# Values of two head pairs from each loaded block of tokens, in one attention stage of a fused block

## The reference, cut to what matters

```python
qkv = x @ w_qkv.T
q, k, v = np.split(qkv, 3, axis=-1)           # 16 heads of 64; q scaled by 64 ** -0.5
# five coarser levels: q and k averaged over pairs of tokens, v summed over pairs
for lvl, (ql, kl, vl) in enumerate(levels):
    # level 0: causal scores inside blocks of 16 tokens
    # level > 0: the odd block of each pair attends to the even block before it
    A = exp(S - S.max(-1))
    Ysum += repeat(A @ v, 2 ** lvl)            # only from the last token of each group on
    Asum += repeat(A.sum(-1), 2 ** lvl)
out = (Ysum / (Asum + 1e-8)) @ w_out.T + b_out
x = x + out
```

## Time and profile before

| what | us |
|---|---|
| runs, median (lowest to highest of 3) | 561.32 (560.02 to 562.15) |
| the profiled execution | 560.87 |
| its span, first to last instruction | 559.1 |
| TensorE busy, 6408 matmul records | 506.0 (91%) |
| TensorE weight loads, beside it | 307.2 (55%) |
| VectorE busy | 425.8 (76%) |
| ScalarE busy | 291.5 (52%) |
| GpSimd busy | 250.6 (45%) |
| attention loop, iterations 0 to 14 | 226.9 to 448 |

### The profile page before, as it was taken

How to read it: one execution, slowest core, us unless ns; L and a number is a source line. 1 busy time by engine, 2 the same in 40 slices (tenths; PEclk the granted TensorE clock), 3 DMA queues, 4 the chain that set the end, 5 groups by cost and what they waited for, 6 DMA issues and landing times.

```text
span 559.1 us, 16575 instructions
## 1 busy us (share of the span) xinstructions
PE 506.0 (91%) x6408; PEld 307.2 (55%) x6408; DVE 425.8 (76%) x979; ACT 291.5 (52%) x624; POOL 250.6 (45%) x294
## 2 busy tenths in 40 slices
PE   6989888888989998999999999999999967989991
PEld 3323232356544544777767777777777755644540
DVE  3396958988747766878899888899878988847762
ACT  3644254254458864666545555546644523448870
POOL 3556677655524454252244443233333335533542
PEclk9999899998999998999999999999999987899997
DMA  6899820000269962100000000000000000169964
GB/s 182 319 426 270 94 25 0 2 0 20 66 194 277 273 211 67 31 3 21 21 21 22 22 21 22 22 21 22 22 20 9 7 2 9 40 184 277 277 215 137
DMA packets 45325, 54.09 MB, mean 97 GB/s; under 512 B 10880, under 2 KB 36416, under 8 KB 44224
## 3 DMA queue, kind: packets, MB, share of 16 engines
q1 hardware_dynamic: 42688, 47.78, 29.6%
q0 software_dynamic: 2560, 5.26, 2.7%
HBM read 43.55 MB, written 9.48 MB: 95 GB/s over the span
## 4 chain that ended last, share of the span: by engine, by line
PE 63%; DVE 22%; issue 6%; DMA 3%; ACT 3%; POOL 2%; SPq 0%; DVEq 0%; POOLq 0%; ACTq 0%
PE psum L1249 9%; PE psum L1748 7%; PE psum L1730 7%; PE psum L1821 5%; PE psum L1800 5%; PE psum L1268 4%; PE psum L1769 3%; PE psum L1256 3%; DVE arena L761 3%; POOL sorted_x L1467 2%; DVE arena L755 2%; PE psum L277 2%; PE psum L278 2%; PE psum L1007 1%; DVE arena L2030 1%
## 5 line engine op out<-in xcount | busy, mean ns | idle before, releaser
L2200 POOL TENSOR_TENSOR arena<-arena 128x512 f32<-128x512 f32 x32 | 40.9, 1302 | 110.6 <-issue 103.9
L1495 POOL DMA_INDIRECT y_tok<-arena,to x48 | 46.6, 971 | 63.3 <-ACT arena L1318 62.1
L1916 ACT ACTIVATE arena<-psum 128x512 f32<-128x512 f32 x64 | 38.1, 597 | 47.4 <-PE psum L1730 44.4
L1730 PE MATMUL psum<-arena 128*128 128x512 f32 x128 | 59.2, 605 | 0.7 <-ACT arena L1899 0.7
L1249 PE MATMUL psum<-experts,arena 128*32 x96 | 50.2, 604 | 1.1 <-ACT arena L1308 1.1
L1249 PE MATMUL psum<-arena 128*32 128x512 f32 x288 | 50.9, 605 | 0.0
L661 POOL TENSOR_TENSOR arena<-arena 128x512 f32<-128x512 f32 x32 | 37.2, 1179 | 27.9 <-DVE arena L761 17.5
L1748 PE MATMUL psum<-arena 128*128 128x128 f32 x384 | 47.5, 278 | 0.8 <-ACT arena L1921 0.8
L1748 PEld LDWEIGHTS psum<-arena 128*128 128x128 f32 x384 | 45.2, 192 | 1.8 <-ACT arena L1921 1.8
L2137 POOL TENSOR_TENSOR arena<-arena 128x256 f32<-128x256 f32 (+4 forms) x75 | 33.6, 447 | 25.9 <-ACT arena L1935 18.9
L1730 PEld LDWEIGHTS psum<-arena 128*128 128x128 f32 x128 | 22.9, 189 | 35.4 <-issue 33.8
(11 more groups left out here) (240 smaller groups left out, 1195.2 us busy)
## 6 DMA issues: line engine op xcount, KB each, us to landing
arena<-in_experts SPq DMA_DIRECT2D x48, 384.0 KB, 4.4
experts<-in_experts SPq DMA_DIRECT2D x8, 1536.0 KB, 17.3
arena<-sorted_x SPq DMA_DIRECT2D x48, 64.5 KB, 3.7
sorted_x<-zeros SPq DMA_DIRECT2D x2, 1536.0 KB, 14.3
arena<-in_w_qkv SPq DMA_DIRECT2D x16, 192.0 KB, 2.8
arena<-y_tok SPq DMA_DIRECT2D x8, 256.0 KB, 3.1
x_tok<-in_x SPq DMA_DIRECT2D x4, 256.0 KB, 4.6
arena<-in_w_out SPq DMA_DIRECT2D x16, 64.0 KB, 1.9
```

What stands on the lines that cost most here:

```text
L1495: pool.indirect_dma_start(out=y_tok, out_offset=bass.IndirectOffsetOnAxis(ap=f_to[:, s:s + 1], axis=0), in_=f_gy[(s + 4) % 8], in_offset=N ...
L1730: pe.matmul(ring("in", n, j)[:, :], b_w[n % 2][:, which * P:which * P + P], x, start=True, stop=True)\
L1916: act.activation((b_q, b_k)[which][:, part * CHUNK:part * CHUNK + CHUNK], src, ACT.Copy, scale=(D_B ** -0.5, 1.0)[which]).then_inc(h["drai ...
L2200: pool.tensor_tensor(b_yn[:, part], b_y[:, part], b_rec[:, part], ALU.mult).then_inc(h["normed"], 1)
```

## The change

TensorE multiplies each loaded block of tokens by the value weights of two neighbouring pairs at once: 12 products of 128x256 for units n and n + 1 (n even), in place of 12 of 128x128 for each unit. They stand before the loop for units 0 and 1, and in the odd iterations 1 to 13 for the next two units; the even iterations have none. An even unit is filled by 5 + 6 banks, an odd one by 5. A drain of a value bank writes two places of `b_v`. There are three places: one for even units, two in turn for odd ones.

The q and k weights of a unit come alone, the value weights of two units in a transfer of their own (`value_weights_in`). `b_yn` is gone: GpSimd multiplies y in place, in `b_y`, except for the last unit, whose y goes to `b_q` (`y_of`). `b_zt` lies in `b_s`, so `divide` now also waits for the turned fine scores. `copy_y` waits for the output products of the unit before in place of its normalisation. `b_odd` keeps only the block of levels 3 to 5 for each batch, and ScalarE's `pack` copies only these levels.

```diff
         def attention_weights_in(sp, n):
-            sp.dma_start(b_w[n % 2].rearrange("p (n c) -> p n c", c=P), w["w_qkv"][n % PAIRS]).then_inc(w_in[n % 2], 16)
+            sp.dma_start(b_w[n % 2].rearrange("p (n c) -> p n c", c=P), w["w_qkv"][n % PAIRS][:, 0:2]).then_inc(w_in[n % 2], 16)
+
+        def value_weights_in(sp, n):
+            two = w["w_qkv"][n % PAIRS:n % PAIRS + 2, :, 2:3].rearrange("u c n d -> c (n u) d")
+            sp.dma_start(b_wv.rearrange("p (u d) -> p u d", d=P), two).then_inc(wv_in, 16)
...
             if k == 0:
-                for n in range(2):
-                    attention_weights_in(sp, n)
+                attention_weights_in(sp, 0)
+                value_weights_in(sp, 0)
+                attention_weights_in(sp, 1)
...
-        b_odd, b_even = carve(TOK // 2), carve(TOK // 2)
-        B_EARLY_AT = used[0]
+        b_odd, b_even = carve(BATCH * P), carve(TOK // 2)
+        b_rec_low, b_max, b_rz = carve(CHUNK), carve(2 * TILES_B), carve(SEQ // 32)
+        B_EARLY_AT = used[0] = max(used[0], F_ROWS_AT + 2 * WROW + 4 * C)
...
-        b_w = [carve(3 * P) for _ in range(2)]
+        b_w, b_wv = [carve(2 * P) for _ in range(2)], carve(2 * P)
...
-        b_v = [carve(TILES_B * P).rearrange("p (i d) -> p i d", d=P) for _ in range(2)]
-        b_max = carve(2 * TILES_B)
-        b_zt, b_rec, b_yn = carve(SEQ), carve(SEQ), carve(SEQ)
-        b_rz = carve(SEQ // 32)
+        b_v = carve(3 * TILES_B * P).rearrange("p (u i d) -> p u i d", i=TILES_B, d=P)
+        b_zt, b_rec = b_s[:, 0:SEQ], [b_rec_low, carve(CHUNK)]
...
-        coarse_of = [[b_rec[:, 0:SEQ // 2], b_yn], [carve(SEQ // 2), carve(SEQ // 2)]]
+        coarse_of = [b_rec, [carve(SEQ // 2), carve(SEQ // 2)]]
...
+        VALUES = TILES_B // 2
+
+        def fills(n):
+            return 5 + (VALUES if n % 2 == 0 else 0)
+
+        def filled_by(n):
+            return 5 * n + VALUES * ((n + 1) // 2)
+
+        def values_of(n):
+            return b_v[:, 0 if n % 2 == 0 else 1 + n // 2 % 2]
...
+        def y_of(n):
+            return b_y if n < LAST else b_q[:, 0:SEQ]
...
             def values(n):
                 b = n // PAIRS
+                pe.wait_ge(wv_in, 16 * (n // 2) + 16)
                 for i in range(TILES_B):
-                    if i % 4 == 0:
-                        bank_free("in", n, 5 + i // 4)
+                    if i % 2 == 0:
+                        bank_free("in", n, 5 + i // 2)
                     x = b_x[:, b * SEQ + i * P:b * SEQ + i * P + P] if i < 8 else \
                         b_even[:, b * CHUNK + (i - 8) * P:b * CHUNK + (i - 8) * P + P]
-                    mm = pe.matmul(ring("in", n, 5 + i // 4)[:, i % 4 * P:i % 4 * P + P], x, b_w[n % 2][:, 2 * P:3 * P],
+                    mm = pe.matmul(ring("in", n, 5 + i // 2)[:, i % 2 * 2 * P:i % 2 * 2 * P + 2 * P], x, b_wv,
                                    start=True, stop=True)
-                    if i % 4 == 3:
+                    if i % 2 == 1:
...
-                pe.wait_ge(h["drained"], IN * n + (8 if rough else 7))
+                pe.wait_ge(h["drained"], filled_by(n // 2 * 2) + (11 if rough else 9))
...
                 if new:
                     project_last(n + 1)
-                if new:
+                if new and n % 2 == 1:
                     values(n + 1)
...
             def pack(b):
-                for level in range(1, LEVELS + 1):
+                for level in range(3, LEVELS + 1):
...
-                    after(act, h["weighed"], 2 * (n - 1) - 1 if j < 7 else 2 * (n - 1))
-                    act.activation(b_v[n % 2][:, 4 * (j - 5):4 * (j - 5) + 4, :], src.rearrange("p (i d) -> p i d", d=P),
+                    after(act, h["weighed"], 2 * (n - 1) - 1 if j < 9 else 2 * (n - 1))
+                    odd, i = 1 + n // 2 % 2, 2 * (j - 5)
+                    act.activation(b_v[:, 0:odd + 1:odd, i:i + 2, :], src.rearrange("p (i u d) -> p u i d", u=2, d=P),
                                    ACT.Copy).then_inc(h["drained"], 1)
...
 
             def copy_y(n):
                 act.wait_ge(h["weighed"], 2 * n + 2)
-                after(act, h["normed"], 2 * n)
-                act.activation(b_y, psum[:, 4 * 512:6 * 512], ACT.Copy).then_inc(h["y_out"], 1)
+                if n < LAST:
+                    after(act, h["o"], 2 * n)
...
             def divide(n):
                 dve.wait_ge(h["summed"], n + 1)
+                dve.wait_ge(h["turned"], 2 * min(n + 1, LAST) + 1)
                 dve.transpose(b_zt, psum[:, 6 * 512:8 * 512]).then_inc(h["z_out"], 1)
...
-                    after(pool, h["o"], 2 * (n - 1) + j + 1)
-                    pool.tensor_tensor(b_yn[:, part], b_y[:, part], b_rec[:, part], ALU.mult).then_inc(h["normed"], 1)
+                    pool.tensor_tensor(y_of(n)[:, part], y_of(n)[:, part], b_rec[j], ALU.mult).then_inc(h["normed"], 1)
...
-                    sp.wait_ge(h["proj"], IN * (n - 2) + IN)
+                    sp.wait_ge(h["proj"], filled_by(n - 2) + 5)
                     attention_weights_in(sp, n)
+                    if n % 2 == 0:
+                        sp.wait_ge(h["proj"], filled_by(n - 1))
+                        value_weights_in(sp, n)
```

45 lines of the change are left out of this document (24 added, 21 removed).

## The result

| what | before | changed kernel |
|---|---|---|
| runs, median (lowest to highest), 4 each | 561.63 (560.02 to 562.15) | 579.41 (578.71 to 580.20) |
| ratio, with its 95% interval | | 1.0315 (1.0281 to 1.0350) |
| the profiled execution | 560.87 | 580.01 |
| its span | 559.1 | 578.1 |
| TensorE busy | 506.0 (91%) | 509.2 (88%) |

The change costs 17.8 us by the medians. One of its six executions took 607.75 us, far above the other five (574.11 to 577.93), and is left out of the ratio. The forecast was 575.4, the range 567.5 to 580; of the first four executions one, of 580.20, lies above it.

A forecast was written before the change was run, and what follows sets the result against it. The prediction took TensorE's products to bound plain iterations, 14.20 of 14.20 us busy. Charges per pair of iterations, 3.8 + 1.3 + 1.3 + 5.6 + 2.8 - 0.4 + 0.1 = 14.5, on 560.87 gave 575.4 us, range 567.5 to 580.

The forecast's parts named there:

- TensorE pays by columns here; the weight loads are hidden.: Value products: equal columns cost equal time, 5.45 us for 12 wide ones; gain taken as 0, at best 0.9 us.
- The iteration lasts 13.3 us.: Plain short iteration, worked on iteration 8: 13.3 us instead of 14.2, saving 0.9 of the 2.8 owed.
- the own wait: In divide, VectorE's transpose of the sums waits for its own transpose of the scores: 0.12 us, bounds 0 and 0.3.
- wait (b): Before the output products of a short iteration, TensorE waits 1.0 us for GpSimd's normalised y, 0.3 more for its second half.
- (d): At the end of a short iteration, add_weights waits 0.3 us for GpSimd's merge, which starts behind the rough exponents.
- Pair 6, +1.9: Iteration 6 and its lengthened neighbour, charged together like those of iteration 8: +1.9 us.
- Iterations 4, 10 and 14 save nothing, +2.8 each: Extra VectorE statistics (10), GpSimd's bias addition (4) and routing work (14) let these short iterations save nothing: +2.8 us each.
- Edits costed at nothing: Two-place value drains, fewer packing copies, split weight transfers, normalising in place and copy_y's moved wait: 0 us.
- Short iterations that give back all: Rival: other engines run ahead in long iterations, so the waits in short ones go: 561 us, chance 6%.
- weight loads that cost time: Rival: value weight loads stand in line, so halving them saves 22.6 us: 552.8 us, chance 5%.
- Clock in all short iterations: Rival: granted clock falls to 0.83 in eight short iterations, 2.3 us each, together 18.7: 594 us, chance 4%.
- The signs: Profile if right: iterations about 17.0 and 13.3, waits before L1841, TensorE busy unchanged within 2 us, 12 value products in 5.5.

The follow-up runs named there:

- narrow_pairs: The changed kernel with each 256-column value product made as two 128-column products on the same block, so blocks are loaded twice: 576.89 us, ratio 1.0300.
- quick_norm: The changed kernel with GpSimd's normalisation of y cut to the first 64 of 512 columns of each half: 574.56 us, ratio 1.0257.
- half_turn: The changed kernel with VectorE's first transpose of divide (of the sums) cut to half its columns: ratio 1.0197.
- half_turn_before: The kernel before the change with VectorE's first transpose of divide cut to half its columns: 563.44 us beside 564.84, ratio 0.9990.
- own_sums: The changed kernel with a place of its own for the turned sums and without divide's wait for VectorE's own transpose: 575.11 us, ratio 1.0276.
- share_only: The kernel before the change with only the shared buffers and the two moved waits, value products untouched: 561.07 us beside 560.83, ratio 1.0009.
- split_values: The changed kernel with the same wide value products halved over two iterations, six blocks in the even and six in the odd one: 565.82 us, ratio 1.0107.
- the repeat: The changed kernel unaltered, measured a second time: 576.47 us beside 559.91 for the kernel before, ratio 1.0293.

## Why the prediction was right, step by step

- **"TensorE pays by columns here; the weight loads are hidden."** Right. 12 wide products took 5.45 us (224.06 to 229.51), as put; `narrow_pairs` gives 0.10 for 12 loads. I took 0 as the gain and kept 0.9 for the low end; 8 x 0.10 = 0.8 by `narrow_pairs` is nearly that end. A long iteration got 2.63 more, not 2.8 (16.84 against 14.21), and so did the stretch before the loop (2.65). Over eight of them this term was 1.4 too high.
- **"The iteration lasts 13.3 us."** 13.56, so 0.65 was saved and not 0.9. The waits in it came out as walked: 0.93 before the output products (1.0 put), their second half 0.37 longer (0.3), 0.27 before L1830 (0.3). The size of three things was off: the own wait was 0.18 and not 0.12; the rough exponents came 0.23 later and not 0.12; and the merge took 2.68 instead of 2.55.
- **What ends an iteration.** The walk was in the right order, but its reader could think that wait (b), 1.0 for GpSimd's normalisation, is the price. `quick_norm` shows that it is not. Only the last link counts, (d), and what leads to it is VectorE; `half_turn` shows that, with `half_turn_before` as its control.
- **Own wait of `divide`, 0.12 each, bounds 0 and 0.3.** `own_sums`: 0.20 to 0.23 in iterations 2, 6 and 8. Inside the bounds.
- **Iteration 0, saving 1.5.** It saved 1.74 (11.32 against 13.06); the sum with the stretch before it was +0.9 instead of +1.3.
- **Iteration 2, saving 1.5.** It saved 1.1 (13.58 against 14.67), so its pair was +1.6 instead of +1.3. The transposes of x had lengthened it by 0.46 (14.67 against 14.21) and not by the 0.62 of their row, and it now ends with the same chain as iteration 8.
- **Pair 6, +1.9.** It was +2.5. Iteration 6 lasted 14.02, 0.46 more than iteration 8, of which 0.25 is a wait at the start of iteration 7 that the prediction lacks: GpSimd packs the next batch's tokens (L2169, 333.69 to 334.92) and TensorE's projection starts at 335.02. `own_sums` and `half_turn` shorten iteration 6 as they do 8. Some 0.2 more is VectorE's later start: its fine maxima begin 0.21 us ahead of TensorE's projections here (320.76, 320.97) and 0.39 in iteration 8, while from them to TensorE's sums it is 12.92 and 12.93. Why it starts later isn't traced.
- **Iterations 4, 10 and 14 save nothing, +2.8 each (10 and 14: +2.6 with their neighbours' bank waits).** Iteration 4: +3.0. Iteration 14: +2.1. Iteration 10: +3.1 with a fall of the clock (next section), some 2.4 without it (14.98 in `narrow_pairs`, where it didn't fall there, against 15.66). Iterations 9 and 13 got 2.1 more each (16.84 against 14.71, 18.19 against 16.11), less than the 2.6 put.
- **Iteration 12, +0.1.** +0.4.
- **Edits costed at nothing.** `share_only`: 0.2 us by the medians, within its interval, though 1.0 in the loop of its one trace. The drains' double places are in `split_values` and cause no wait of note there; the transfers landed in 2.8 us as before. Those of the value weights were issued some 21 us before use and not over 25 (349.50, used at 370.42), since the load of the output weights stood ahead of them on SyncE.
- **Rivals.** Short iterations that give back all (561), and weight loads that cost time (552.8), are out. Clock in all short iterations (594): no, in one of them.
- **The signs.** Iterations of 16.84 and 13.56, the waits before L1841, the value products and the clock above 0.95 (0.99 from 230 to 440 us) came as put. TensorE's busy time rose by 3.2 us, not under 2: 1.3 of it are the output products of iteration 10 at half clock and 0.5 the router products at half clock in the last layer. The remaining 1.4 I can't place; a busy sum includes modelled ends.

The terms make 14.5 and the pairs of the table 15.5, but not because each term was right. Too low were the pairs 1 and 2 (0.3), 3 and 4 (0.2), 5 and 6 (0.6), 7 and 8 (0.1), 9 and 10 (0.5; the clock took 0.5 to 0.7 there) and 11 and 12 (0.3); too high the start (0.4) and 13 and 14 (0.5). Under them lies the same kind of offset: eight long iterations priced 1.4 too high, short ones that saved less than put. That these nearly cancel is luck; that TensorE pays in full and VectorE's chain keeps the short ones from giving it back is not. The medians say 16.6 to 17.8; what lies between these and the 15.5, 1 to 2 us, is not in the attention loop, and what of it is scatter of the other layers is left open. The first measurement, 579.4, is only 0.6 inside the range, the repeat 3.5.

## What to carry to other kernels

Moving work of a full engine between iterations at an equal sum is not free: the long iterations pay it in full, the short ones give back only down to the next chain, and the other engine's idle time of the long iteration (4.85 us here) can't be used if what it waits for stands behind the added work. The long iterations' share follows from the table, the short ones' limit from `half_turn` and `quick_norm`. Before merging products to save weight loads, compare the records' time per column (0.118 us for 128, 0.227 for 256, 0.454 for 512): if it is proportional, there is nothing to save. And a wait named in a timeline is not its price: cut the operation it waits for, and see whether the end of the iteration moves.
